# Three in-order lists re-ordered in the opening of a transformer block kernel: a weight piece, an activation and an up product change places

## The chip, the cores and the metric

The kernel runs on one core of a Trainium2 chip. The metric is device time in microseconds of one execution. Engines are TensorE (matmuls and transposes), VectorE, ScalarE (activations) and GpSimd; SyncE issues most transfers. Each engine works through its own list in order, and semaphores tie the lists together.

## The reference

x is 1024 x 256 in float32. The block is a feed-forward part, an attention part and the same feed-forward part once more:

```
x = x + 0.5 * ffn(layernorm(x))
x = x + retention(layernorm(x))     # 16 heads, rotation, decay, group norm, silu gate
x = x + 0.5 * ffn(layernorm(x))

ffn(h): gate = silu((h @ fp8(gate_w)) * gate_s);  up = (h @ fp8(up_w)) * up_s
        return ((gate * up) @ fp8(down_w)) * down_s      # 256 -> 768 -> 256
```

fp8(w) means that the weights are rounded to float8 e4m3 and then used in float32.

## The kernel before, in words

Rows of x are eight tiles of 128 (n = 0 to 7), in two groups of four (g = 0, 1). The change lies in the first feed-forward part, in the first 20 us.

**Weights.** They come in eight pieces (q = 0 to 7): gate and up in three cuts (columns 0 to 128, 128 to 384, 384 to 768; gate has q = 0, 2, 4 and up q = 1, 3, 5), down in two halves (6, 7). Each piece is rounded on the chip in five steps: VectorE's grid_step(q) (L670), grid_clip(q) (L676) and grid_add(q) (L682); a subtract(q), on VectorE for q = 0 and 3 (L687) and on GpSimd for the others (L309); and ScalarE's to_weights(q) (L404), which writes the weights that TensorE uses. The ring `grid` has three slots.

**h.** Per tile: statistics on VectorE (L705, L709), the root rstd on GpSimd (`roots`, L316 and L318, one call for tiles 4 to 7), shift = -mean * rstd on VectorE (shift_rows, L694), and the norm on ScalarE (norm_act, L412). TensorE turns h (turn_h, L1121) into a bank; ScalarE takes the high part hhi (split_h, L445) and VectorE the rest hlo (rest_h, L735).

**Products.** Product j is a pair (group g, 128 columns i), in the order (0,0) (0,1) (0,2) (1,0) (1,1) (1,2) and then (0,3) and on. gate_up(j) is two halves, "gate" and "up", of four matmuls each (hhi twice, then hlo twice; L1167; product 0 has its own order, L1143). silu(j) on ScalarE (L455) reads the gate half; fuse_up(j) on VectorE (L752) multiplies it with the up half; split_f(j) on ScalarE (L463) and rest_f(j) on VectorE (L760) or GpSimd (L324) split the product for the down matmuls (L1195). Each half has two banks, so the gate of j waits for silu(j - 2) and the up of j for fuse_up(j - 2):

```
if j >= 2:
    pe.wait_ge(silu_done if m == "gate" else fuse_done, j - 1)
```

The first product of group 1 (j = 3) waits for all four hhi parts, and for all four hlo parts ahead of its third matmul. The lists of the engines are written out by hand, call after call; nothing else sets the order. The changed lines lie in the list of ScalarE (L557 to L567), of VectorE (L893 to L904) and of TensorE (L1378 to L1381).

Of the kernel before, what the change touches and what calls it, by code (L numbers as in the profile page):

```python
# [64 lines left out]
def subs(n):  # L65

    on_pool = sum(q < n for q in SUB_ON_POOL)
    return n - on_pool, on_pool
# [14 lines left out]
def rests(n):  # L83

    on_pool = sum(j < n for j in REST_ON_POOL)
    return n - on_pool, on_pool
# [41 lines left out]
def macaron(nc, x, w_qkv, w_g, w_proj, gn_w, gn_b, gate_w, up_w, down_w, gate_s, up_s, down_s,  # L128
            rotation_t, mask_t, out):
    with ExitStack() as ctx:  # L130
# [66 lines left out]
        def piece(base, q):  # L197

            m, a, b = PIECES[q]
            if m == "down":  # L200
                return base[:, a * C:b * C].rearrange("p (k n) -> p k n", k=b - a)
            return base.rearrange("p (k n) -> p k n", k=KC)[:, :, a:b]

        def packed(ring, q):
            m, a, b = PIECES[q]
            k, n = (b - a, C) if m == "down" else (KC, b - a)
            return ring[:, q % GRID_SLOTS, 0:k * n].rearrange("p (k n) -> p k n", k=k)
# [51 lines left out]
        def roots_until(n):  # L259

            return next(i for i, (a, b) in enumerate(root_groups) if a <= n < b) + 1
# [135 lines left out]
        def _(act):  # L397
            def to_weights(q):

                if q in SUB_ON_POOL:  # L400
                    act.wait_ge(sub_pool, subs(q + 1)[1])
                else:
                    act.wait_ge(sub_dve, subs(q + 1)[0])
                nc.scalar.activation(piece(wr[PIECES[q][0]][:, :], q), packed(grid, q), ACT.Copy,  # L404
                                     scale=W_SCALE).then_inc(w_ready, 1)

            def norm_act(n):

                act.wait_ge(shift_done, roots_until(n))
                if n >= TH:  # L410
                    act.wait_ge(turned, n - TH + 1)
                nc.scalar.activation(h[:, n % TH, :], xt[:, n, :], ACT.Identity, scale=rstd[:, n:n + 1],  # L412
                                     bias=shift[:, n:n + 1]).then_inc(h_act, 1)
# [33 lines left out]
            def silu(j):  # L447

                if j == 0:
                    act.wait_ge(vec_done, 1)  # L450
                act.wait_ge(gate_done, j + 1)
                if j >= 2:
                    act.wait_ge(fuse_done, j - 1)
                i = PRODUCTS[j][1]
                nc.scalar.activation(gact[:, j % 2, :], pairs[j // (NG * NI)][j % 2][0][:, :], ACT.Silu,  # L455
                                     scale=gate_col[:, i:i + 1]).then_inc(silu_done, 1)
# [100 lines left out]
            turned_vectors()  # L557
            to_weights(2)
            silu(0)
            norm_act(4)  # L560
            norm_act(5)
            norm_act(6)
            norm_act(7)
            to_weights(3)
            split_h(1, 0)
            split_h(1, 1)
            silu(1)  # L567
            silu(2)
            to_weights(4)
            split_f(0)  # L570
# [93 lines left out]
        def _(dve):  # L664
            def grid_step(q):

                dve.wait_ge(raw_in[q], 16)
                if q >= GRID_SLOTS:
                    dve.wait_ge(w_ready, q - GRID_SLOTS + 1)
                dve.tensor_scalar(packed(grid, q).bitcast(U32), piece(raws[PIECES[q][0]], q).bitcast(U32),  # L670
                                  EXP_BITS, HALF_BIT, ALU.bitwise_and, ALU.bitwise_or).then_inc(exp_done, 1)

            def grid_clip(q):

                dve.wait_ge(exp_done, q + 1)
                dve.tensor_scalar(packed(grid, q), packed(grid, q), GRID_MIN, LIFT, ALU.max, ALU.mult).then_inc(clip_done, 1)  # L676

            def grid_add(q):

                dve.wait_ge(clip_done, q + 1)  # L680
                w = piece(raws[PIECES[q][0]], q)
                dve.tensor_tensor(w, w, packed(grid, q), ALU.add).then_inc(added, 1)  # L682

            def subtract(q):

                dve.wait_ge(added, q + 1)
                dve.tensor_tensor(packed(grid, q), piece(raws[PIECES[q][0]], q), packed(grid, q),  # L687
                                  ALU.subtract).then_inc(sub_dve, 1)

            def shift_rows(g):  # L690

                a, b = root_groups[g]
                dve.wait_ge(rstd_done, g + 1)
                dve.scalar_tensor_tensor(out=shift[:, a:b], in0=mv[:, a:b, 0], scalar=-1.0, in1=rstd[:, a:b],  # L694
                                         op0=ALU.mult, op1=ALU.mult).then_inc(shift_done, 1)
# [43 lines left out]
            def fuse_up(j):  # L739

                dve.wait_ge(up_done, j + 1)
                dve.wait_ge(silu_done, j + 1)
                if j == 0:
                    dve.wait_ge(vec_done, 1)
                last = j - FUSE_SLOTS
                if last >= 0:
                    if last in REST_ON_POOL:
                        dve.wait_ge(flo_pool, rests(last + 1)[1])
                    else:
                        dve.wait_ge(flo_dve, rests(last + 1)[0])  # L750
                i = PRODUCTS[j][1]
                dve.scalar_tensor_tensor(out=fuse[:, j % FUSE_SLOTS, :], in0=pairs[j // (NG * NI)][j % 2][1][:, :], scalar=up_col[:, i:i + 1],  # L752
                                         in1=gact[:, j % 2, :], op0=ALU.mult, op1=ALU.mult).then_inc(fuse_done, 1)
# [139 lines left out]
            grid_clip(3)  # L893
            grid_step(4)
            grid_add(3)
            shift_rows(2)
            subtract(3)
            fuse_up(0)
            grid_clip(4)
            grid_step(5)  # L900
            grid_add(4)
            rest_h(1, 0)
            rest_h(1, 1)
            fuse_up(1)  # L904
            grid_clip(5)
            fuse_up(2)
            grid_add(5)
# [187 lines left out]
        def _(pe):  # L1095
# [5 lines left out]
            def turn_h(g):  # L1101

                n0 = (g if g < NG else g + NG) * TH
                if g == 1:
                    pe.wait_ge(hlo_done, KC)
                if g == 2:
                    pe.wait_ge(rs_done, NT)
                    pe.wait_ge(v_done, NT)
                    pe.wait_ge(kvm_done, NT - 1)
                if g == 3:  # L1110
                    pe.wait_ge(gd_done, NT)
                    pe.wait_ge(x2_done, NT - 1)
                for t in range(TH):
                    if g == 0 and t >= 2:
                        keep_busy(1)
                    if n0 + t in NORM_ON_ACT:
                        pe.wait_ge(h_act, norms(n0 + t + 1)[1])
                    else:
                        pe.wait_ge(h_done, norms(n0 + t + 1)[0])
                    for k in range(KC):  # L1120
                        mm = pe.matmul(turn[g][k][:, t * P:(t + 1) * P], h[:, (n0 + t) % TH, k * P:(k + 1) * P], ident,  # L1121
                                       is_transpose=True, start=(t == 0), stop=True, skip_group_check=True)
                    mm.then_inc(turned, 1)
# [24 lines left out]
            def gate_up(j, parts=("gate", "up")):  # L1148

                g, i = PRODUCTS[j]  # L1150
                if i == 0:
                    pe.wait_ge(hhi_done, KC * (g + 1))
                if j == NG * NI:
                    pe.wait_ge(hlo_done, KC * (NG + 1))
                elif j == NG * NI + 1:
                    pe.wait_ge(sc_masked, HG * NT)
                for m in parts:
                    if g < NG:
                        pe.wait_ge(w_ready, PIECES_NEEDED[i] - (m == "gate"))
                    if j >= 2:  # L1160
                        pe.wait_ge(silu_done if m == "gate" else fuse_done, j - 1)
                    dst = pairs[g // NG][j % 2][m == "up"]
                    for half in (hhi, hlo):
                        if half is hlo:
                            pe.wait_ge(hlo_done, KC * (g + 1))
                        for k in range(KC):
                            mm = pe.matmul(dst[:, :], wr[m][:, k * I + i * P:k * I + (i + 1) * P], half[:, k, g % NG, :],  # L1167
                                           start=(k == 0 and half is hhi), stop=(k == KC - 1 and half is hlo))
                    mm.then_inc(gate_done if m == "gate" else up_done, 1)
# [207 lines left out]
            first_gate_up()  # L1377
            gate_up(1, ("gate",))  # L1378
            gate_up(2, ("gate",))
            turn_h(1)  # L1380
            gate_up(1, ("up",))  # L1381
            gate_up(2, ("up",))
            gate_up(3, ("gate",))
            gate_up(3, ("up",))
# [158 lines left out]
```

## Time and profile before

| | us |
|---|---|
| median of 3 runs | 155.21 |
| lowest and highest | 155.19, 155.21 |
| the profiled execution | 155.3 |
| its span, first to last instruction | 153.5 |
| granted TensorE clock, share of full | 1.00 |

Times of the trace are microseconds from the start of the span. A timeline row has the start, the time to the last end, the engine, the line, the operation, what is written and read, the count, and in brackets the idle time ahead of it with what ended it. Several instructions in a row of one kind are merged (x2, x4), and the records of neighbours overlap a little.

### The profile page before, as it was taken

The numbers are of one execution on the slowest core, as the hardware profiler recorded it, in microseconds if no ns is written. First come the engines' busy times: TensorE is split into PE (matmuls) and PEld (weight loads), VectorE is DVE, ScalarE is ACT, GpSimd is POOL, SyncE is SP. The second block draws the span as 40 slices with busy tenths as digits, with TensorE's granted clock in tenths as the row PEclk, the third lists the DMA queues.
The fourth block names the chain that finished last, engine by engine and source line by source line (L and its number), as shares of the span: only waits on it lengthen the run. The fifth ranks groups of instructions, "written<-read, shape, count | busy, mean of one in ns | idle before, by whom it ended". The sixth has DMA issues, their size and how long they took to land.

```text
span 153.5 us, 3712 instructions
## 1 busy us (share of the span) xinstructions
PE 147.2 (96%) x1327; PEld 117.4 (76%) x1327; DVE 121.4 (79%) x271; ACT 85.2 (56%) x203; POOL 68.5 (45%) x76
## 2 busy tenths in 40 slices
PE   5999899999999999998999999999999999999992
PEld 2366588788989696967686969698877788888991
DVE  0797999999799485859688888899755999566784
ACT  2385998677232453547475656657676648453310
POOL 3447244775891700283845748573978220000000
PEclk9999999999999999999999999999999999999999
DMA  4999502903000000000000000000000000002114
GB/s 112 339 354 306 214 0 31 361 27 121 15 0 0 4 0 4 0 4 0 4 2 0 6 0 6 0 4 0 4 2 0 0 4 0 0 0 68 34 36 139
DMA packets 7009, 8.47 MB, mean 55 GB/s; under 512 B 448, under 2 KB 5712, under 8 KB 6992
## 3 DMA queue, kind: packets, MB, share of 16 engines
q1 hardware_dynamic: 6816, 8.16, 16.0%
q8 instruction: 11, 0.18, 0.5%
q10 hardware_dynamic: 176, 0.07, 0.4%
q14 instruction: 6, 0.05, 0.1%
HBM read 7.19 MB, written 1.05 MB: 54 GB/s over the span
## 4 chain that ended last, share of the span: by engine, by line
PE 74%; POOL 10%; DVE 6%; issue 4%; ACT 3%; DMA 2%; POOLq 0%; ACTq 0%; DVEq 0%
PE bank L1167 23%; PE bank L1195 14%; PE bank L1223 9%; POOL grstd L340 6%; PE bank L1280 5%; PE bank L1236 5%; PE bank L1250 4%; PE bank L1364 3%; PE bank L1309 3%; DMA xt<-in_L_attn_x 2%; POOL rstd L318 2%; PE bank L1262 2%; DVE stats L705 2%; PE bank L1296 1%; PE bank L1341 1%
## 5 line engine op out<-in xcount | busy, mean ns | idle before, releaser
L1167 PE MATMUL bank<-hh,up_r 128*128 128x512 f32 x92 | 25.5, 401 | 0.1
L1167 PE MATMUL bank<-hh,gate_r 128*128 128x512 f32 x92 | 25.6, 401 | 0.0
L1195 PE MATMUL bank<-down_r,fhi 128*128 128x256 f32 x96 | 24.3, 291 | 0.0
L340 POOL TENSOR_TENSOR grstd<-gve,neg_half 128x16 f32<-128x16 f32 x8 | 23.3, 2908 | 0.7
L1195 PE MATMUL bank<-down_r,flo 128*128 128x256 f32 x96 | 23.4, 281 | 0.0
L455 ACT ACTIVATE gact<-bank,vec 128x512 f32<-128x512 f32 x24 | 16.3, 684 | 9.0 <-PE bank L1167 8.1
L463 ACT ACTIVATE fhi<-fuse 128x512 fp32r<-128x512 f32 x24 | 14.6, 624 | 10.8 <-DVE fuse L752 10.8
L1167 PEld LDWEIGHTS bank<-hh,up_r 128*128 128x128 f32 x92 | 16.8, 188 | 4.3 <-issue 0.6
L1167 PEld LDWEIGHTS bank<-hh,gate_r 128*128 128x128 f32 x92 | 16.9, 188 | 4.0 <-ACT gate_r L404 0.4
L1195 PEld LDWEIGHTS bank<-down_r,fhi 128*128 128x128 f32 x96 | 18.1, 188 | 0.7 <-issue 0.2
L1195 PEld LDWEIGHTS bank<-down_r,flo 128*128 128x128 f32 x96 | 18.1, 188 | 0.6 <-issue 0.2
L809 DVE TENSOR_TENSOR sc<-bank,msk 128x384 f32<-128x384 f32 x32 | 16.5, 549 | 1.9 <-PE bank L1280 1.9
L752 DVE SCALAR_TENSOR_TENSOR fuse<-bank,vec,gact 128x512 f32<-128x512 f32 x24 | 17.6, 744 | 0.2
L760 DVE TENSOR_TENSOR flo<-fuse,fhi 128x512 fp32r<-128x512 f32 x20 | 14.1, 727 | 3.1 <-ACT fhi L463 3.0
L316 POOL TENSOR_SCALAR ve<-mv 128x1 f32<-128x1 f32 (+3 forms) x15 | 4.8, 318 | 24.8 <-DVE mv L709 24.7
L1223 PE MATMUL bank<-wqkv,h 128*128 128x512 f32 x32 | 15.3, 600 | 0.4 <-ACT h L471 0.4
L309 POOL TENSOR_TENSOR grid<-raw,grid 128x768 f32<-128x768 f32 (+2 forms) x6 | 10.7, 1778 | 9.8 <-DVE raw L682 9.8
L330 POOL TENSOR_TENSOR x<-yd,xt 128x256 f32<-128x256 f32 x8 | 6.3, 802 | 11.2 <-DVE yd L772 11.2
L789 DVE TENSOR_TENSOR rc<-bank,raw 128x512 f32<-128x512 f32 x8 | 5.5, 690 | 7.1 <-PE bank L1223 7.1
L318 POOL TENSOR_TENSOR rstd<-ve,neg_half 128x1 f32<-128x1 f32 (+3 forms) x15 | 10.4, 692 | 1.2
L772 DVE TENSOR_TENSOR yd<-bank,ds 128x256 f32<-128x256 f32 x16 | 6.6, 420 | 4.3 <-PE bank L1195 4.2
L1280 PEld LDWEIGHTS bank<-qT,kM 32*128 32x128 f32 x256 | 7.9, 186 | 2.0 <-issue 1.5
(90 smaller groups left out, 285.6 us busy)
## 6 DMA issues: line engine op xcount, KB each, us to landing
raw<-in_rotation SPq DMA_DIRECT2D x1, 1536.0 KB, 7.5
out<-xt SPq DMA_DIRECT2D x8, 128.0 KB, 1.8
raw<-in_L_ffn_down_w SPq DMA_DIRECT2D x2, 384.0 KB, 7.4
wqkv<-in_L_attn_w_qkv SPq DMA_DIRECT2D x1, 768.0 KB, 9.3
xt<-in_L_attn_x SPq DMA_DIRECT2D x2, 256.0 KB, 3.7
xt<-in_L_attn_x SPq DMA_DIRECT2D x1, 512.0 KB, 5.4
raw<-in_rotation SPq DMA_DIRECT2D x1, 512.0 KB, 3.5
raw<-in_L_ffn_gate_w SPq DMA_DIRECT2D x1, 384.0 KB, 6.2
```

Source lines behind the costliest of these rows:

```text
L309: pool.tensor_tensor(packed(grid, q), piece(raws[PIECES[q][0]], q), packed(grid, q), ALU.subtract).then_inc(sub_pool, 1)
L318: pool.tensor_tensor(rstd[:, a:b], ve[:, a:b], neg_half[:, 0:b - a], ALU.pow).then_inc(rstd_done, 1)
L340: pool.tensor_tensor(grstd[:, c % 2], gve[:, :], neg_half[:, :], ALU.pow).then_inc(grstd_done, 1)
L455: nc.scalar.activation(gact[:, j % 2, :], pairs[j // (NG * NI)][j % 2][0][:, :], ACT.Silu, scale=gate_col[:, i:i + 1]).then_inc(silu_done, 1)
L463: nc.scalar.activation(fhi[:, g % NG, i, :], fuse[:, j % FUSE_SLOTS, :], ACT.Copy).then_inc(fhi_done, 1)
L752: dve.scalar_tensor_tensor(out=fuse[:, j % FUSE_SLOTS, :], in0=pairs[j // (NG * NI)][j % 2][1][:, :], scalar=up_col[:, i:i + 1], in1=gact[ ...
L760: dve.tensor_tensor(flo[:, g % NG, i, :], fuse[:, j % FUSE_SLOTS, :], fhi[:, g % NG, i, :].bitcast(F32), ALU.subtract).then_inc(flo_dve, 1)
L809: dve.tensor_tensor(sc[:, r], b_sc[r][:, 0:KC * SP].rearrange("p (k t) -> p k t", t=SP), causal.unsqueeze(1).to_broadcast([P, KC, SP]), AL ...
L1167: mm = pe.matmul(dst[:, :], wr[m][:, k * I + i * P:k * I + (i + 1) * P], half[:, k, g % NG, :], start=(k == 0 and half is hhi), stop=(k == ...
L1195: mm = pe.matmul(downs[d][:, 0:C], half[:, g % NG, i, t * P:(t + 1) * P], wr["down"][:, i * C:(i + 1) * C], start=(i == 0 and half is fhi) ...
L1223: mm = pe.matmul(b_qk[:, :], h2[:, c % 2, k, :], wqkv[:, k, 0:2 * C], start=(k == 0), stop=(k == KC - 1))
L1280: mm = pe.matmul(b_sc[r][:, k * SP + half * P:k * SP + P + half * HP], kM[at, k, half].rearrange("p m s -> p (m s)"), qT[at, c % 2, k, hal ...
```

## The change

On ScalarE silu(1) and to_weights(3) go ahead of the norms of tiles 4 to 7. On VectorE subtract(3) goes ahead of shift_rows(2), and fuse_up(1) ahead of grid_step(5), grid_add(4) and the two rest_h. On TensorE the up half of product 1 goes ahead of turn_h(1). Nothing is added or taken away.

```diff
@@ ScalarE
             to_weights(2)
             silu(0)
+            silu(1)
+            to_weights(3)
             norm_act(4)
             norm_act(5)
             norm_act(6)
             norm_act(7)
-            to_weights(3)
             split_h(1, 0)
             split_h(1, 1)
-            silu(1)
             silu(2)
             to_weights(4)
             split_f(0)
@@ VectorE
             grid_clip(3)
             grid_step(4)
             grid_add(3)
+            subtract(3)
             shift_rows(2)
-            subtract(3)
             fuse_up(0)
             grid_clip(4)
+            fuse_up(1)
             grid_step(5)
             grid_add(4)
             rest_h(1, 0)
             rest_h(1, 1)
-            fuse_up(1)
             grid_clip(5)
             fuse_up(2)
             grid_add(5)
@@ TensorE
             first_gate_up()
             gate_up(1, ("gate",))
             gate_up(2, ("gate",))
+            gate_up(1, ("up",))
             turn_h(1)
-            gate_up(1, ("up",))
             gate_up(2, ("up",))
             gate_up(3, ("gate",))
```

## Rows read from the trace of the kernel before

**Rows 1.** The page: busy time of each engine (share of the span)

```profile
PE 147.2 (96%) x1327; PEld 117.4 (76%) x1327; DVE 121.4 (79%) x271; ACT 85.2 (56%) x203; POOL 68.5 (45%) x76
```

**Rows 2.** The chain that ended last: start, us, what

```profile
13.53 1.38 POOL rstd L318
14.94 0.17 DVE shift L694
...
...
17.79 16.25 PE bank L1167 x68
```

**Rows 3.** Busy time by windows, one of three that are alike

```profile
24.00:28.00 4.00, 4.00 (x19) 3.26 (x18) 4.00 (x7) 2.52 (x4) 1.94 (x2) 1.00 0.49 112
```

**Rows 4.** Timeline around the up half of product 8

```profile
29.20 1.40 DVE L752 SCALAR_TENSOR_TENSOR fuse<-bank,vec,gact 128x512 f32<-128x512 f32 x2
...
30.05 0.30 PEld L1167 LDWEIGHTS bank<-hh,up_r 128*128 128x128 f32 x2 [0.34 <-issue]
```

**Rows 5.** Timeline of VectorE, 13 to 21.5 us

```profile
13.33 0.68 DVE L682 TENSOR_TENSOR raw<-raw,grid 128x512 f32<-128x512 f32 x1
...
15.02 0.69 DVE L687 TENSOR_TENSOR grid<-raw,grid 128x512 f32<-128x512 f32 x1
15.62 0.74 DVE L752 SCALAR_TENSOR_TENSOR fuse<-bank,vec,gact 128x512 f32<-128x512 f32 x1
16.28 0.55 DVE L676 TENSOR_SCALAR grid<-grid 128x768 f32<-128x768 f32 x1
...
17.22 0.95 DVE L682 TENSOR_TENSOR raw<-raw,grid 128x768 f32<-128x768 f32 x1
18.38 1.29 DVE L735 SCALAR_TENSOR_TENSOR hh<-bank,hh 128x512 fp32r<-128x512 f32 x2 [0.21 <-ACT hh L445]
...
20.24 0.55 DVE L676 TENSOR_SCALAR grid<-grid 128x768 f32<-128x768 f32 x1
20.71 0.74 DVE L752 SCALAR_TENSOR_TENSOR fuse<-bank,vec,gact 128x512 f32<-128x512 f32 x1
```

**Rows 6.** Timeline of TensorE, 13 to 20 us

```profile
13.24 2.13 PE L1167 MATMUL bank<-hh,gate_r 128*128 128x512 f32 x8
...
17.79 1.21 PE L1167 MATMUL bank<-hh,up_r 128*128 128x512 f32 x4
```

**Rows 7.** Timeline of ScalarE, 15 to 23.5 us

```profile
15.14 2.08 ACT L412 ACTIVATE h<-xt,shift,rstd 128x256 f32<-128x256 f32 x4 [1.33 <-DVE shift L694]
17.12 0.62 ACT L404 ACTIVATE up_r<-grid 128x512 fp32r<-128x512 f32 x1
17.75 1.09 ACT L445 ACTIVATE hh<-bank 128x512 fp32r<-128x512 f32 x2
...
20.14 0.85 ACT L404 ACTIVATE gate_r<-grid 128x768 fp32r<-128x768 f32 x1 [0.16 <-POOL grid L309]
...
21.94 1.50 ACT L455 ACTIVATE gact<-bank,vec 128x512 f32<-128x512 f32 x2
```

**Rows 8.** Timeline of GpSimd: its subtracts of pieces 4, 5 and 6

```profile
18.25 1.86 POOL L309 TENSOR_TENSOR grid<-raw,grid 128x768 f32<-128x768 f32 x1 [3.34 <-DVE raw L682]
22.39 2.24 POOL L309 TENSOR_TENSOR grid<-raw,grid 128x768 f32<-128x768 f32 x1 [2.29 <-DVE raw L682]
...
28.88 2.10 POOL L309 TENSOR_TENSOR grid<-raw,grid 128x768 f32<-128x768 f32 x1 [0.89 <-DVE raw L682]
```

**Rows 9.** Timeline of VectorE: two instructions that start under those subtracts

```profile
24.34 0.71 DVE L670 TENSOR_SCALAR grid<-raw 128x768 uint32<-128x768 uint32 x1
...
30.52 0.88 DVE L676 TENSOR_SCALAR grid<-grid 128x768 f32<-128x768 f32 x1
```

**Rows 10.** Timeline of VectorE and GpSimd: instructions inside a root

```profile
6.93 0.43 DVE L682 TENSOR_TENSOR raw<-raw,grid 128x256 f32<-128x256 f32 x1
...
112.35 2.90 POOL L340 TENSOR_TENSOR grstd<-gve,neg_half 128x16 f32<-128x16 f32 x1
...
113.02 0.42 DVE L857 TENSOR_TENSOR go<-ga,sg 128x256 f32<-128x256 f32 x1 [0.49 <-ACT ga L536]
```

## The prediction

> **What bounds the kernel now.** I read the page first: TensorE is busy for nearly the whole span and VectorE for four fifths of it [rows 1]. Shares of the span don't say which of them sets the pace of one stage, so I went to the chain of work that ended last. The reader should see two things there [rows 2]. Until about 15 us the chain runs through GpSimd's root (the power that makes rstd of tiles 4 to 7) and VectorE's shift; and from 17.79 us on 68 gate and up matmuls follow one another. TensorE looks like the only bound from there.
>
> The busy time by windows corrects this: in 24 to 28 us VectorE too is busy 4.00 of 4.00 us [rows 3]. (Two more windows, to 36 us, look alike.) Then I looked for the places where TensorE waits inside its dense stretch. At 30.05 us its weight load comes after 0.34 us without one, put down to "issue" [rows 4]. The code tells more: the up half of product 8 waits for fuse_done 7, so for fuse_up(6). That is the first of the two fuses from 29.20 us; one takes 0.74, so it ends at 29.94, and the load follows 0.11 us later. From 24 to 37 us the two engines are tied: TensorE can't run ahead of VectorE's list. A gain on TensorE counts only if VectorE is also earlier, and a delay of VectorE goes through at product 8.
>
> **The change, part by part.** No instruction is added or removed, no DMA moved; three in-order lists change. I replay each with the durations of before. A VectorE instruction starts about 0.08 us before the record of its predecessor ends, so one step is 0.60 for a 512 subtract (15.02 to 15.62), 0.66 for a fuse, 0.47 for a clip or a grid step (the two take 16.28 to 17.22), and an add of 768 takes 0.95 [rows 5].
>
> *subtract(3) ahead of shift_rows(2).* grid_add(3) ends at 14.01 (13.33 + 0.68). The subtract runs 14.04 to 14.73, inside the gap in which VectorE waits for the root, which ends at 14.90 [rows 2, 5]. It costs nothing there, and the shift stays at 14.94. Without that cover it would cost 0.60.
>
> *ScalarE: silu(1) and to_weights(3) ahead of norms 4 to 7.* The eight gate matmuls of products 1 and 2 start at 13.24 [rows 6]. Four take about 0.93 start to start, the last record 0.39: product 1's gate is done near 14.33. silu(1) starts at 14.37, to_weights(3) 0.59 later, at 14.95; it takes 0.62 [rows 7] and ends at 15.57. The norms start at about 15.54 and not 15.14, 0.40 late. ScalarE's wait of 1.3 us covers the rest of the two moved instructions. What is queued behind: the norms end 0.40 later, the two split_h (1.09 together) start at 18.15 and end at 19.25 [rows 7].
>
> *TensorE: up of product 1 ahead of turn_h(1).* It needs the weight piece of 15.57, starts at 15.65, and, as the first product after a pause, takes the 1.21 us of its row of before [rows 6]: done at 16.86. This fills idle time ahead of the turn. But gate 3, first product of h's second half, needs both hhi parts (19.25) and, for its third matmul, both hlo.
>
> *VectorE: fuse_up(1) ahead of grid_step(5) and grid_add(4).* fuse_up(0) comes 0.60 earlier, at 15.02, clip(4) at 15.68 to 16.23. Then VectorE waits for product 1's up: 0.65 us of new idle time. fuse_up(1) 16.89, step(5) 17.55, grid_add(4) 18.02 to 18.97. Before, that add started at 17.22: it is 0.80 later. rest_h follows at 18.89 and ends at 20.18 (two take 1.29), and clip(5) comes up at 20.10, where it was at 20.24 [rows 5]. In sum VectorE is 0.14 ahead here, but in another order.
>
> First result: hlo is ready at 20.18, and gate 3's third matmul starts at 20.2 to 20.3. Before, gate 3 started at 19.76 and so had its third matmul near 20.22. The up product that was moved into the pause (0.93) gives TensorE nothing by 20.3, since the stall reappears ahead of hhi and hlo.
>
> Second result: GpSimd's subtract(4) waits for grid_add(4). It ran 18.25 to 20.11 and now runs 19.05 to 20.91 [rows 8]. That puts it under clip(5). What happens then is in the trace: grid_step(6) started at 24.34 under GpSimd's subtract(5), which ended at 24.63 (22.39 + 2.24), and itself ended at 25.05; clip(7) started at 30.52 under GpSimd's subtract(6), which ended at 30.98, and took 0.88 to 31.40 [rows 8, 9]. Both end 0.42 after GpSimd, while a free clip takes 0.55 [rows 5]. So clip(5) ends at 20.91 + 0.42 = 21.33, and fuse_up(2) starts at 21.25 and not at 20.71: **0.54 late**.
>
> Is the delay given back? By ScalarE's list no: to_weights(4) waits for subtract(4), 0.80 later, at 20.94; silu(3) came 1.80 after it (21.94 after 20.14) [rows 7], so 22.74 to 23.41. VectorE's list brings fuse_up(3) to 22.84 + 0.54 = 23.38, the silu to 23.44; then fuse_up(4) 24.10 and step(6) 24.76. GpSimd's subtract(5) follows grid_add(5) and so is 0.54 late too, to 25.17; step(6) runs under it again and ends at 25.59 and not at 25.05. That is 0.54 once more, and the small slack in front of fuse_up(4) is gone in the same wait. From there VectorE has no idle time to give back [rows 3], and ScalarE and GpSimd, fed by it, keep their places relative to it. fuse_up(6) ends at 30.48, up of product 8 starts at 30.59. With nothing gained on TensorE the shift is 0.54. All later work hangs on these lists; the rotation loads hang on the subtracts and have long to spare.
>
> **Sum.** 0 (subtract) + 0 (TensorE's moved product) + 0.54 (VectorE's list) = +0.54 us. The profiled execution took 155.3 us (a span of 153.5 and 1.8 around it), so 155.84; it lies 0.09 above the median, 155.21, so as a median 155.75, said as 155.7. Bounds of the sum: if clip(5) isn't held, only ScalarE's route is left: fuse_up(4) at 24.10 is 0.42 late, step(6) then runs free after an earlier subtract(5) and ends at 25.31, +0.26, which is the lower end.
>
> **The rivals.**
>
> *A, the clip is not held, or the delay is partly given back* (no change). For it: the hit depends on 0.8 us of overlap, that is on fuse_up(1)'s wait for TensorE, and I composed six steps. Against: the margin is large. Time: +0.26 down to 0, so 155.2 to 155.5.
>
> *B, TensorE is the bound after all* (faster). If VectorE's lag is absorbed before product 8, TensorE keeps what its fuller pause gives: 0.93 for the up product less the norms' 0.40 is 0.53, 154.7; with the hlo wait at its earliest (second hhi at 19.25, rest_h 0.65, so 19.95 and not 20.22) it is 0.27, 154.9. For it: the chain of before is TensorE from 17.79 on [rows 2]. Against: the wait at 30.05 [rows 4]. It decides once VectorE reaches fuse_up(6) earlier than at 29.20.
>
> *C, GpSimd's root holds up subtract(3)* (slower still). The root runs 13.53 to 14.90, and the subtract reads two SBUF operands. If it has to wait for the root, it ends at 15.5, to_weights(3) at 16.2 and everything behind is 0.6 later: +1.14, 156.35. Against: the gated product at 113.02, also two SBUF operands, started inside GpSimd's 2.90 us root of 112.35 and took 0.42; grid_add(0) at 6.93, inside another root, took 0.43 [rows 10]. A root that is under way held neither. For it: here the root has itself waited for grid_add(3) and so reads just when the subtract starts. The Trainium skill, "SBUF — State Buffer", "Who interferes with whom", says that a VectorE instruction with two SBUF inputs contends with a GpSimd instruction that reads SBUF, and that the first one keeps the shared pair "for the whole instruction". By it subtract(3) would wait until 14.90 and rival C's time would come out; the row at 113.02 speaks against the rule for this operation.
>
> **How the numbers follow.** Forecast 0.50 (155.5 to 156.0); A 0.22; B 0.14; C 0.14. The likeliest gives 155.7. The range 155.0 to 156.35 takes in A, the forecast and C's point, and leaves out most of B and what lies beyond C. About 0.2%, 0.31 us, is what a measurement of this kernel can tell from no change. Faster: B, 0.14. Same: A and 0.07 of the forecast's low end, 0.29. Slower: 0.43 of the forecast and C, 0.57.
>
> **What would show it.** In the changed profile: subtract(3) at 14.04 with 0.7 us; ScalarE's norms from about 15.5; idle time of about 0.65 us on VectorE ahead of the second fuse; GpSimd's subtract(4) at 19.05; clip(5) stretched from 0.55 to over 1.1 us; the weight load of product 8's up near 30.6. The prediction is wrong if grid_add(4) ends ahead of 18.3 (no overlap with clip(5)), if the third matmul of gate 3 starts well before 20.2 and the wait at product 8 is gone (B), or if subtract(3) is stretched to 15.5 (C).

## The result and the profile after

The changed kernel takes 155.82 us (median of 6 runs, 155.53 to 156.22) against 155.18 us for the kernel before (6 runs): +0.64 us, ratio 1.0045 with a 95% interval of 1.0031 to 1.0058. On a second occasion, beside other kernels, it was 155.72 against 155.16: +0.56 us, ratio 1.0034, interval 1.0022 to 1.0047. It is slower, by about the 0.54 us forecast. Two executions on record, one of the kernel before (183.52 us) and one of a kernel of the experiments (289.5 us), were disturbed; the intervals leave them out, and without them the differences below that rest on those medians move by at most 0.03 us.

The profiled execution happens to be the fastest of the six, 155.53 us with a span of 153.7. That is no contradiction: VectorE's first statistics start at 4.03 us, when the first rows of x have landed, and started at 4.33 in the trace of before. The opening varied by 0.3 us between these two, so traces have to be compared from a common event. I take the start of the first gate matmul of product 1: 13.24 before [rows 6], 12.92 after. All else is read as a distance from it. To compare a time of the trace after with one of before, add 0.32.

VectorE's timeline of the changed kernel:

```profile
13.74 0.69 DVE L687 TENSOR_TENSOR grid<-raw,grid 128x512 f32<-128x512 f32 x1
14.64 0.16 DVE L694 SCALAR_TENSOR_TENSOR shift<-mv,rstd 128x4 f32<-128x4 f32 x1 [0.20 <-POOL rstd L318]
14.76 0.75 DVE L752 SCALAR_TENSOR_TENSOR fuse<-bank,vec,gact 128x512 f32<-128x512 f32 x1
15.42 0.55 DVE L676 TENSOR_SCALAR grid<-grid 128x768 f32<-128x768 f32 x1
16.64 0.75 DVE L752 SCALAR_TENSOR_TENSOR fuse<-bank,vec,gact 128x512 f32<-128x512 f32 x1 [0.66 <-PE bank L1167]
17.30 0.55 DVE L670 TENSOR_SCALAR grid<-raw 128x768 uint32<-128x768 uint32 x1
17.77 0.95 DVE L682 TENSOR_TENSOR raw<-raw,grid 128x768 f32<-128x768 f32 x1
18.64 1.28 DVE L735 SCALAR_TENSOR_TENSOR hh<-bank,hh 128x512 fp32r<-128x512 f32 x2
19.84 1.21 DVE L676 TENSOR_SCALAR grid<-grid 128x768 f32<-128x768 f32 x1
20.97 0.74 DVE L752 SCALAR_TENSOR_TENSOR fuse<-bank,vec,gact 128x512 f32<-128x512 f32 x1
...
24.57 0.74 DVE L670 TENSOR_SCALAR grid<-raw 128x768 uint32<-128x768 uint32 x1
```

The subtract of piece 3 (first row) is free inside the gap. The second fuse (16.64) waits 0.66 us for the up product. The clip of piece 5 (19.84) takes 1.21 us, where before it took 0.55 [rows 5]. The last row is grid_step(6), held a second time.

GpSimd's timeline shows what holds them:

```profile
13.23 1.37 POOL L318 TENSOR_TENSOR rstd<-ve,neg_half 128x4 f32<-128x4 f32 x1
18.80 1.83 POOL L309 TENSOR_TENSOR grid<-raw,grid 128x768 f32<-128x768 f32 x1 [4.20 <-DVE raw L682]
22.65 2.24 POOL L309 TENSOR_TENSOR grid<-raw,grid 128x768 f32<-128x768 f32 x1 [2.02 <-DVE raw L682]
```

subtract(4) ends at 18.80 + 1.83 = 20.63, the clip at 19.84 + 1.21 = 21.05, 0.42 later. subtract(5) ends at 24.89, grid_step(6) at 25.31, again 0.42 later.

ScalarE's timeline: silu(1), to_weights(3), the norms, the two high parts, and to_weights(4) after 1.15 us of waiting:

```profile
14.15 0.69 ACT L455 ACTIVATE gact<-bank,vec 128x512 f32<-128x512 f32 x1 [0.65 <-PE bank L1167]
14.73 0.62 ACT L404 ACTIVATE up_r<-grid 128x512 fp32r<-128x512 f32 x1
15.25 2.06 ACT L412 ACTIVATE h<-xt,shift,rstd 128x256 f32<-128x256 f32 x4
17.85 1.08 ACT L445 ACTIVATE hh<-bank 128x512 fp32r<-128x512 f32 x2 [0.53 <-PE bank L1121]
...
20.66 0.85 ACT L404 ACTIVATE gate_r<-grid 128x768 fp32r<-128x768 f32 x1 [1.15 <-POOL grid L309]
```

TensorE's timeline around the turn, and its weight load for product 8's up:

```profile
12.92 2.13 PE L1167 MATMUL bank<-hh,gate_r 128*128 128x512 f32 x8
15.41 1.19 PE L1167 MATMUL bank<-hh,up_r 128*128 128x512 f32 x4 [0.36 <-ACT up_r L404]
...
18.98 0.74 PE L1167 MATMUL bank<-hh,gate_r 128*128 128x512 f32 x2 [0.24 <-ACT hh L445]
19.98 0.73 PE L1167 MATMUL bank<-hh,gate_r 128*128 128x512 f32 x2 [0.25 <-DVE hh L735]
```

```profile
30.31 0.75 PEld L1167 LDWEIGHTS bank<-hh,up_r 128*128 128x128 f32 x4 [0.70 <-issue]
```

The up product fills the pause, and the pause comes back as two stalls inside product 3's gate, which is cut in two (x2 and x2). The wait ahead of product 8's up grew from 0.34 to 0.70 us [rows 4]. Its distance from the common event was 30.05 - 13.24 = 16.81 us and is 30.31 - 12.92 = 17.39: **+0.58 us**, the loss of the kernel. The chain that ended last tells the same:

```profile
17.30 0.55 DVE grid L670
17.85 0.87 DVE raw L682
18.72 0.85 DVE hh L735 x2
19.57 0.27 issue
19.84 1.21 DVE grid L676
21.05 0.66 DVE fuse L752
21.71 0.88 DVE raw L682
22.59 0.07 issue
22.65 2.25 POOL grid L309
```

Before, TensorE's 68 matmuls stood here [rows 2]. Now the chain goes through VectorE's add, the clip and GpSimd's subtract, and on through ScalarE and VectorE, until it comes back to TensorE at 30.34 us.

### The profile page after: what moved, and what is told of

Its sections match the earlier page's. It is cut to its first block, busy times and chain, and to the rows that moved or that the text cites. A ratio compares the mean times of both kernels' runs of the same rounds, so it can differ in the third digit from the quotient of the medians.

```text
span 153.7 us, 3712 instructions
## 1 busy us (share of the span) xinstructions
PE 146.8 (95%) x1327; PEld 117.0 (76%) x1327; DVE 122.1 (79%) x271; ACT 85.1 (55%) x203; POOL 68.5 (45%) x76
## 4 chain that ended last, share of the span: by engine, by line
PE 71%; POOL 9%; DVE 8%; issue 4%; ACT 4%; DMA 2%; POOLq 0%; DVEq 0%; ACTq 0%
PE bank L1167 17%; PE bank L1195 14%; PE bank L1223 9%; POOL grstd L340 6%; PE bank L1280 5%; PE bank L1236 5%; PE bank L1250 4%; PE bank L1364 3%; PE bank L1309 3%; DMA xt<-in_L_attn_x 2%; DVE raw L682 2%; PE bank L1262 2%; POOL grid L309 1%; PE bank L1296 1%; PE bank L1143 1%
## 5 line engine op out<-in xcount | busy, mean ns | idle before, releaser
L1223 PE MATMUL bank<-wqkv,h 128*128 128x512 f32 x32 | 15.3, 600 | 0.4 <-ACT h L471 0.4
```

The source lines that it names most:

```text
L1223: mm = pe.matmul(b_qk[:, :], h2[:, c % 2, k, :], wqkv[:, k, 0:2 * C], start=(k == 0), stop=(k == KC - 1))
```

## The experiments

All were timed beside the kernel before on one chip (medians of it: 155.18 beside the first row, then 155.22, 155.16 and 155.26 in the three groups). "Distance" is that from the first gate matmul of product 1 to the weight load of product 8's up, in the profile of each, less the 16.81 of before. The time is a median over 6 to 12 executions and the distance is read from one trace; the two should agree if the whole effect lies in this stage. A second distance, to the first matmul of the attention part (L1223, at 44.67 us before), is within 0.02 us of the first in every row, so what is read at product 8 is still there when the feed-forward part is done.

| kernel | median less before, us | ratio and interval | distance, us | clip(5), us |
|---|---|---|---|---|
| changed kernel | +0.64 | 1.0045 (1.0031 to 1.0058) | +0.58 | 1.21 |
| changed kernel again | +0.56 | 1.0034 (1.0022 to 1.0047) | +0.58 | 1.21 |
| only subtract(3) early | +0.04 | 1.0003 (0.9994 to 1.0011) | +0.03 | 0.55 |
| only ScalarE's order, subtract(3) early | +0.45 | 1.0029 (1.0020 to 1.0037) | +0.42 | 0.55 |
| changed, fuse_up(1) back behind rest_h | +0.49 | 1.0034 (1.0022 to 1.0046) | +0.48 | 0.55 |
| changed, fuse_up(1) behind grid_step(5) | +0.16 | 1.0010 (1.0000 to 1.0020) | +0.11 | 0.90 |
| changed, fuse_up(1) behind grid_add(4) | -0.27 | 0.9983 (0.9973 to 0.9993) | -0.24 | 0.55 |
| the same again | -0.32 | 0.9983 (0.9974 to 0.9991) | -0.23 | 0.55 |
| changed, fuse_up(2) ahead of clip(5) | +0.25 | 1.0012 (1.0003 to 1.0022) | +0.31 | 0.57 |
| fuse_up(1) behind grid_add(4), silu(1) behind the norms | -0.46 | 0.9973 (0.9963 to 0.9984) | -0.32 | 0.55 |

**subtract(3) alone** (on the kernel before)

```diff
             grid_add(3)
+            subtract(3)
             shift_rows(2)
-            subtract(3)
             fuse_up(0)
```

> The kernel before with one edit: subtract(3) ahead of shift_rows(2). Theory (the subtract runs free in the gap under GpSimd's root): subtract 0.7 us, the root still 1.37 us, fuse_up(0) and grid_add(4) 0.6 us earlier, but rest_h still waits for hhi, so the time stays within 0.1 us of before. Rival C (subtract and root hold each other up): the subtract is stretched to over 1.3 us, or the root to over 1.8 us, and the time is 0.2 to 0.6 us longer.

The time is the same. The subtract starts 0.51 us after the root, inside it, and neither record is stretched: 0.69 us here as before [rows 5], and 1.38 for the root as before [rows 2].

```profile
13.78 0.69 DVE L687 TENSOR_TENSOR grid<-raw,grid 128x512 f32<-128x512 f32 x1
```

```profile
13.27 1.38 POOL L318 TENSOR_TENSOR rstd<-ve,neg_half 128x4 f32<-128x4 f32 x1
```

Rival C is out, and with it, for this root, the rule that the prediction takes from the Trainium skill, "SBUF — State Buffer", "Who interferes with whom".

**ScalarE's order** (with the early subtract; TensorE as before, fuse_up(1) as before)

```diff
             silu(0)
+            silu(1)
+            to_weights(3)
             norm_act(4)
...
             norm_act(7)
-            to_weights(3)
             split_h(1, 0)
             split_h(1, 1)
-            silu(1)
             silu(2)
```

> The kernel before with ScalarE's new order and the early subtract(3) alone; TensorE's list and the rest of VectorE's as before. Theory: TensorE's moved up product is worth nothing, since hhi comes 0.4 to 0.5 us late either way, and VectorE, which waits for hhi, is late by as much: +0.4 to +0.5 us, the same as the kernel that has TensorE's move as well (+0.5). Rival (the moved up product is worth its 0.93 us or part of it): over +0.8 us here.

It loses by itself: +0.45. VectorE's rest_h stands idle for hhi far longer than the 0.21 us of before [rows 5]:

```profile
18.76 1.29 DVE L735 SCALAR_TENSOR_TENSOR hh<-bank,hh 128x512 fp32r<-128x512 f32 x2 [1.30 <-ACT hh L445]
```

**fuse_up(1) back behind rest_h** (the three lists as changed otherwise)

```diff
             grid_clip(4)
-            fuse_up(1)
             grid_step(5)
             grid_add(4)
             rest_h(1, 0)
             rest_h(1, 1)
+            fuse_up(1)
             grid_clip(5)
```

> The changed kernel with fuse_up(1) put back behind rest_h on VectorE; ScalarE, TensorE and subtract(3) as changed. Theory (two separate costs: the place of fuse_up(1), and the norms that come 0.4 us later): GpSimd's subtract(4) is long over when clip(5) starts, so no held clip, but VectorE now waits about 1.6 us for hhi and its list is about 0.36 us late; total +0.3 to +0.4 us over before. Rival (the held clip is the whole loss): +0.0 or a gain. Rival (ScalarE's and TensorE's order is the whole loss): as the changed kernel, +0.64.

ScalarE's norms, then VectorE's rest_h and clip(5):

```profile
15.89 2.07 ACT L412 ACTIVATE h<-xt,shift,rstd 128x256 f32<-128x256 f32 x4
```

```profile
19.11 1.29 DVE L735 SCALAR_TENSOR_TENSOR hh<-bank,hh 128x512 fp32r<-128x512 f32 x2 [0.92 <-ACT hh L445]
...
20.98 0.55 DVE L676 TENSOR_SCALAR grid<-grid 128x768 f32<-128x768 f32 x1
```

+0.49, a little above the range written down. In this trace the norms start 2.40 us after the common event (13.49 here), against 1.90 before, so hhi was 0.5 and not 0.4 us late; that accounts for the distance of +0.48. It is a trace of the slowest of the six executions (156.19 us), so it need not account for the median. VectorE waited 0.92 us for hhi and not the 1.6 written down. The clip is free, and the kernel is slow all the same. So the held clip is not the whole story. Against the kernel above this one adds TensorE's moved up product alone: +0.49 with it, +0.45 without, with overlapping intervals. As long as VectorE takes fuse_up(1) only behind rest_h, the move on TensorE is worth nothing.

**fuse_up(1) behind grid_step(5)**

```diff
             grid_clip(4)
-            fuse_up(1)
             grid_step(5)
+            fuse_up(1)
             grid_add(4)
```

> The changed kernel with fuse_up(1) between grid_step(5) and grid_add(4). Theory of the held clip: grid_add(4) ends near 18.5, GpSimd's subtract(4) near 20.45, clip(5) is held to 20.87 and not 21.33, so the total is 0.0 to +0.15 us over before, some 0.5 us better than the changed kernel, though VectorE does the same work in nearly the same order. Rival (what costs is that VectorE waits for the up product, or the norms' delay): the total stays near +0.5 to +0.64.

One instruction step later than in the changed kernel, and 0.4 to 0.5 us of the loss is gone. The profile, and the distance in the table, come from an execution of their own:

> One more look at the kernel with fuse_up(1) between grid_step(5) and grid_add(4), for its profile. Theory of the held clip: clip(5) takes 0.9 to 1.1 us, that is between the free 0.55 and the changed kernel's 1.21, and ends 0.42 us after GpSimd's subtract(4).

It is one more execution, of 155.38 us. Here are GpSimd and VectorE:

```profile
18.57 1.83 POOL L309 TENSOR_TENSOR grid<-raw,grid 128x768 f32<-128x768 f32 x1 [3.74 <-DVE raw L682]
```

```profile
16.87 0.75 DVE L752 SCALAR_TENSOR_TENSOR fuse<-bank,vec,gact 128x512 f32<-128x512 f32 x1 [0.21 <-PE bank L1167]
...
19.91 0.90 DVE L676 TENSOR_SCALAR grid<-grid 128x768 f32<-128x768 f32 x1
```

The subtract ends at 20.40, the clip at 20.81: 0.41 later. A smaller overlap, a shorter record, the same distance between the two ends.

**fuse_up(1) behind grid_add(4)**

```diff
             grid_clip(4)
-            fuse_up(1)
             grid_step(5)
             grid_add(4)
+            fuse_up(1)
             rest_h(1, 0)
```

> The changed kernel with fuse_up(1) behind grid_add(4) and ahead of rest_h. Theory: grid_add(4) ends near 17.6, GpSimd's subtract(4) near 19.5, ahead of clip(5) at about 19.95, which is free (0.55 us); fuse_up(2) starts 0.29 us earlier than before, fuse_up(6) too, TensorE has 0.15 to 0.25 us in hand at product 8; total -0.2 to -0.3 us against before. Rival (TensorE and ScalarE changes lose by themselves): +0.2 or more. Rival B of the prediction (TensorE is the only bound): about -0.5.

> The kernel with fuse_up(1) behind grid_add(4) once more, on another chip allocation and beside the kernel above: -0.2 to -0.3 us against before.

Faster than the kernel before as well as the changed one: -0.27 and, the second time, -0.32. VectorE's timeline, then TensorE's load for product 8's up and the up halves of product 8 and of the product two later:

```profile
16.24 0.95 DVE L682 TENSOR_TENSOR raw<-raw,grid 128x768 f32<-128x768 f32 x1
17.11 0.74 DVE L752 SCALAR_TENSOR_TENSOR fuse<-bank,vec,gact 128x512 f32<-128x512 f32 x1
18.36 1.29 DVE L735 SCALAR_TENSOR_TENSOR hh<-bank,hh 128x512 fp32r<-128x512 f32 x2 [0.51 <-ACT hh L445]
19.57 0.55 DVE L676 TENSOR_SCALAR grid<-grid 128x768 f32<-128x768 f32 x1
```

```profile
29.36 0.87 PEld L1167 LDWEIGHTS bank<-hh,up_r 128*128 128x128 f32 x4
```

```profile
29.57 1.10 PE L1167 MATMUL bank<-hh,up_r 128*128 128x512 f32 x4
...
34.10 1.16 PE L1167 MATMUL bank<-hh,up_r 128*128 128x512 f32 x4
```

The fuse now stands where VectorE would wait for hhi, and waits for nothing itself. GpSimd's subtract(4), 17.27 to 19.11, is over 0.46 us before the clip. Product 8's up carries no idle time: at this place TensorE is the bound again. The distance needs care here. A load that doesn't wait starts 0.21 us ahead of its first matmul (29.36, 29.57), one that waits 0.03 (30.05, 30.08 before). So product 8's matmuls themselves come only 0.06 us earlier than before, counted from the common event (12.79 here). The rest of the -0.24 shows at the next up half that waits for VectorE: 34.10 here and 34.78 before, 0.23 earlier by the same count. This kernel and the one with fuse_up(1) behind rest_h differ in the place of one fuse, and lie 0.76 us apart. TensorE's moved up product has its worth here: it lets fuse_up(1) run ahead of rest_h without a wait.

**The clip behind a fuse** (the changed kernel; a clip has one operand, in SBUF, and a fuse has one in SBUF and one in a bank)

```diff
             rest_h(1, 1)
-            grid_clip(5)
             fuse_up(2)
+            grid_clip(5)
             grid_add(5)
```

> The changed kernel with fuse_up(2) ahead of grid_clip(5), so that VectorE has something to do that reads only one operand from SBUF while GpSimd's subtract(4) runs. Theory of the held clip: clip(5) takes about 0.6 us and not 1.21, fuse_up(2) comes 1.1 us and grid_add(5) 0.55 us earlier than in the changed kernel; silu(3) stays where it is, since to_weights(4) still comes late, so VectorE gains only about 0.26 us there: total +0.3 to +0.4 us over before. But rest_f(0) then comes up in the same instant as GpSimd's subtract(5); if GpSimd is first, rest_f(0) is held to the end of that subtract and the total is over +1.5 us. Rival (clip(5)'s long record is a wait for something else, not GpSimd's subtract): clip(5) stays long or the total stays at +0.64.

GpSimd's two subtracts, then VectorE:

```profile
19.11 1.85 POOL L309 TENSOR_TENSOR grid<-raw,grid 128x768 f32<-128x768 f32 x1 [4.04 <-DVE raw L682]
22.45 2.35 POOL L309 TENSOR_TENSOR grid<-raw,grid 128x768 f32<-128x768 f32 x1 [1.49 <-DVE raw L682]
```

```profile
20.15 0.74 DVE L752 SCALAR_TENSOR_TENSOR fuse<-bank,vec,gact 128x512 f32<-128x512 f32 x1
20.81 0.57 DVE L676 TENSOR_SCALAR grid<-grid 128x768 f32<-128x768 f32 x1
21.41 0.96 DVE L682 TENSOR_TENSOR raw<-raw,grid 128x768 f32<-128x768 f32 x1
22.40 0.69 DVE L760 TENSOR_TENSOR flo<-fuse,fhi 128x512 fp32r<-128x512 f32 x1
23.57 1.41 DVE L752 SCALAR_TENSOR_TENSOR fuse<-bank,vec,gact 128x512 f32<-128x512 f32 x2 [0.48 <-ACT gact L455]
```

subtract(4) ran 19.11 to 20.96 here, 5.90 us after the common event (13.21), as late as in the changed kernel (5.88). The fuse ran under it at its usual 0.74. The clip met only its last 0.15 us and took 0.57; it still ends 0.42 after it. With subtract(4) as late as before and most of the overlap taken away, the stretch is gone, so the long record of clip(5) comes from its overlap with GpSimd's subtract.

The last row shows why only half of the loss is gone: 0.48 us of waiting for silu(3), which hangs behind to_weights(4) and so behind subtract(4). fuse_up(3) comes no earlier than in the changed kernel: 10.36 us after the common event, 10.32 there, 9.60 before. What the freed clip gives is an earlier grid_add(5) and with it an earlier subtract(5), which is over at 24.80, before grid_step(6) starts at 24.89: that step is free here (0.55) and was held in the changed kernel (0.74). So the late subtract(4) costs by two routes, through the clip on VectorE and through to_weights(4) on ScalarE, and taking one away leaves the other.

The race I feared ended well: rest_f(0) came up 0.05 us before GpSimd's subtract(5), at 22.45, and wasn't held.

**silu(1) behind the norms** (on the kernel with fuse_up(1) behind grid_add(4))

```diff
             silu(0)
-            silu(1)
             to_weights(3)
...
             norm_act(7)
+            silu(1)
             split_h(1, 0)
```

> The best kernel so far (fuse_up(1) behind grid_add(4)) with silu(1) moved from ahead of to_weights(3) and the norms to behind the norms, where ScalarE waits 0.53 us for TensorE. Theory: to_weights(3) then starts when subtract(3) ends, the norms and hhi come about 0.2 us earlier; fuse_up(1) waits for silu(1) and so starts about 0.4 us later, which takes back half of it at rest_h; a further 0.1 us at most over the best kernel, total -0.3 to -0.4 us against before. Rival (fuse_up(1) is late enough to push rest_h back by more than hhi gains): -0.1 to -0.25 us.

-0.46 against before; the best median. Beside it the kernel that it was made from had -0.32, and the intervals of the two overlap (0.9963 to 0.9984, 0.9974 to 0.9991), so a gain over that one isn't settled; the distance gives it 0.09 us. Its time lies 0.06 beyond the range written down.

## Why the prediction was right, point by point

**What bounds the stage.** VectorE and TensorE are tied from 24 to 37 us, and product 8's up is where VectorE's lateness goes through. The times and the distances of the ten rows agree within 0.14 us, most within 0.06: nearly nothing was lost or given back behind that point. A gain does not go through there in full: in the two faster kernels the matmuls of product 8 moved by 0.06 and 0.15 us only, and the rest showed at the up half of 34.78 us, the next that waits for VectorE.

**subtract(3) costs nothing.** Right: 13.74 + 0.32 is 14.06 (forecast 14.04), alone +0.04 us, within noise.

**ScalarE, norms 0.40 late.** Measured 2.33 us after the common event against 1.90: 0.43.

**TensorE gains nothing.** Right: the idle time is back at hhi and hlo. Product 3's third matmul came at 19.98 + 0.32 = 20.30, the upper end of the 20.2 to 20.3 forecast.

**VectorE's new wait, GpSimd's subtract(4), the held clip.** Forecast and measured (+ 0.32): wait 0.65 and 0.66; subtract(4) 19.05 to 20.91 and 19.12 to 20.95; clip(5) ends 21.33 and 21.37; fuse_up(2) 21.25 and 21.29; grid_step(6) ends 25.59 and 25.63; product 8's up 30.59 and 30.63.

**The sum.** +0.54 forecast; +0.58 by distance, +0.64 and +0.56 by the medians. The events of that list came 0.04 us late because silu(1) started at 14.15 + 0.32 = 14.47 and not at 14.37, and product 1's up at 15.73 and not at 15.65; subtract(4) then started 0.07 late, and its record was 0.03 shorter (1.83 against 1.86). One step was further off: fuse_up(3) came at 23.24 + 0.32 = 23.56, forecast 23.44, and grid_step(6) started 0.13 late. It did no harm, since grid_step(6) then waited under GpSimd's subtract(5) anyway. That the sum comes so close owes something to this second hold.

**What the prediction didn't say.** It priced ScalarE's order at nothing. In the changed kernel that is true only because VectorE comes late to rest_h anyway: the cover is the loss itself. Take the held clip away by putting fuse_up(1) back, and the norms' 0.43 us appears in full (+0.45 and +0.49). So the changed kernel has two costs that hide each other, not one. The prediction's lower bound, +0.26 where clip(5) isn't held, held for the swap of clip and fuse (+0.25, distance +0.31) and not in general. Even there it was partly luck: the end of grid_step(6) came 0.42 us late and not 0.26, and a grid_add behind it gave 0.10 back (1.39 us against 1.49 before), since it too stood under an instruction of GpSimd and the overlap had shrunk. The gain that the change could give was there as well, -0.27 to -0.32 us, two lines away in VectorE's list; the prediction looked for a gain only in rival B, on TensorE.

**The rivals.** A: not what happened, the clip was held in both profiles of the changed kernel. B: the wait at product 8 grew and did not vanish. C: excluded by the subtract alone.

## What to carry to other kernels

When two engines are tied, an instruction moved ahead on one list must be asked two things: does it wait where it now stands, and what does its wait push back that feeds a third engine. fuse_up(1) put two lines lower (behind the add that releases GpSimd, ahead of the wait for hhi) turned +0.6 us into -0.3 us with the same work. Put the instruction that starts another engine's long work ahead of one that may wait, and fill real waits with what is ready.

Compare traces of runs that differ by tenths from a common event; the first transfer alone moved the opening by 0.3 us here, enough to make the profiled run of a slower kernel look nearly as fast as before.

## What the runs showed of the hardware

A VectorE clip or grid step of 128 x 768, which takes 0.55 us free, ends 0.41 to 0.43 us after the GpSimd subtract under which it starts, with overlaps from 0.15 to 0.79 us: records of 0.57, 0.74, 0.90 and 1.21 us. With an overlap of 0.02 to 0.03 us (grid_step(6) of the faster kernels) it took its free 0.55. A fuse, with one operand in SBUF and one in a bank, runs under the same subtract at 0.74 us.

The grid_add of 128 x 768, with two operands in SBUF, is held as well, here by GpSimd's rest_f in the kernel before, first GpSimd's row and then VectorE's:

```profile
26.69 1.30 POOL L324 TENSOR_TENSOR flo<-fuse,fhi 128x512 fp32r<-128x512 f32 x1 [2.05 <-ACT fhi L463]
```

```profile
27.31 1.49 DVE L682 TENSOR_TENSOR raw<-raw,grid 128x768 f32<-128x768 f32 x1
```

It ends 0.81 us after the rest_f and takes 0.95 free. GpSimd seems to be held in turn: its subtract(5) started at 22.39 under VectorE's rest_f(0) (22.23 to 22.92) and took 2.24 us [rows 8], where subtract(4) took 1.86.

GpSimd's root, also an instruction with two SBUF operands, does not hold VectorE's 512 subtract that starts 0.51 us after it (0.69 us, the root 1.37 to 1.38 in every run). The root itself starts under grid_add(3) in every run. Roots of one, two and three columns took 0.57, 0.72 and 0.88 us, so one of four would take about 1.03 (an estimate from these); the 0.34 beyond that fits a wait for grid_add(3), but no run here takes that add away.

The Trainium skill, "SBUF — State Buffer", "Who interferes with whom", states the rule behind the first of these: only a pair of ports shared by VectorE and GpSimd makes them contend, and whoever is first has it to itself. By it tensor_scalar, the operation of clip and grid step, can take the pair in a two-port mode although it has one input, an instruction with two SBUF inputs contends with a GpSimd instruction that reads SBUF, and one with at most one SBUF input outside the two-port modes doesn't contend. The records above agree: clip and step (0.57 to 1.21 us) and add (1.49) are held, the fuse (0.74) isn't. No run here shows the mode itself; that a clip of 768 takes 0.55 us and an add of 768 takes 0.95 goes with it. The root departs from the "for the whole instruction" of the Trainium skill: it was under way and the subtract was not held. That the root reads its few operands at its start and then needs the ports no more would explain it, but no run here shows when it reads.
